# A recommender tower on one core: the first block of samples gets its own split of the pair units, the sums get freer groups, and the order is planned anew

## What is computed

```python
e = jnp.stack([tbl_0[ids[:, 0]], ..., tbl_39[ids[:, 39]]], axis=1)   # (2048, 40, 64)
viW = jnp.einsum('bpd,pde->bpe', vi, W)      # vi = e[:, i_idx], W is (780, 64, 64)
z = jnp.einsum('bpe,bpe->bp', viW, vj)       # (2048, 780)
h = jnp.concatenate([z, dense_ctx], axis=1)  # 16 dense columns more: 796
h = jnp.maximum(h @ W_top1 + b_top1, 0.0)    # 512
h = jnp.maximum(h @ W_top2 + b_top2, 0.0)    # 256
y = h @ W_top3                               # 1
```

## Time and profile before

| | |
|---|---|
| median of 3 runs | 1356.27 us (1356.18 to 1361.23) |
| profiled execution: from its first to its last instruction (the span) | 1195.2 us |
| difference of the median to that span | 161.1 us |
| PE busy | 1177.7 us (99%) |
| DVE busy | 1003.0 us (84%) |
| ACT busy | 966.7 us (81%) |
| POOL busy | 774.4 us (65%) |
| TensorE clock granted | full (1.000) all along |
| bytes moved | 79.73 MB, 67 GB/s over the span |

### The profile page before, as it was taken

One profiled execution on the slowest core, in us unless ns is written; L12 is line 12 of the kernel. 1 busy time (PEld: TensorE's weight loads), 2 busy tenths in 40 slices (PEclk: granted clock), 3 DMA queues, 4 the chain that ended last, 5 costly groups with the idle time before them and its releaser, 6 DMA issues.

```text
span 1195.2 us, 23954 instructions
## 1 busy us (share of the span) xinstructions
PE 1177.7 (99%) x6248; PEld 457.7 (38%) x6248; DVE 1003.0 (84%) x915; ACT 966.7 (81%) x7477; POOL 774.4 (65%) x1026
## 2 busy tenths in 40 slices
PE   7999999999999999999999999999999999999999
PEld 2433333333434343333434343433343434343333
DVE  7898999999588888999877878889978778888960
ACT  1295989899476799999687879999969899999971
POOL 8888883687656556677755557887765556634320
PEclk9999999999999999999999999999999999999999
DMA  7143232222222222222222222222222222211100
GB/s 211 38 148 78 65 75 65 70 72 72 57 56 68 56 67 73 68 67 70 71 55 63 60 64 65 71 63 78 73 57 59 59 66 63 66 45 55 49 10 0
DMA packets 68480, 79.73 MB, mean 67 GB/s; under 512 B 15308, under 2 KB 46028, under 8 KB 68216
## 3 DMA queue, kind: packets, MB, share of 16 engines
q1 hardware_dynamic: 48752, 58.10, 16.6%
q0 software_dynamic: 19456, 19.96, 9.3%
q10 hardware_dynamic: 136, 0.14, 0.1%
HBM read 78.14 MB, written 0.01 MB: 65 GB/s over the span
## 4 chain that ended last, share of the span: by engine, by line
PE 89%; DVE 5%; issue 4%; ACT 1%; POOL 1%; DMA 0%; SPq 0%; DVEq 0%; ACTq 0%; POOLq 0%
PE u_ps L1007 30%; PE u_ps L1003 23%; PE z_ps L1032 16%; PE turn_ps L1063 7%; PE turn_ps L965 3%; PE u_ps L997 3%; PE turn_ps L958 2%; DVE fprod L1172 2%; PE turn_ps L1073 2%; PE u_ps L1063 2%; DVE acts L1128 1%; DVE zb L1180 1%; DVE rprod_A L1163 1%; PE u_ps L1073 1%; ACT rprod_A L1234 1%
## 5 line engine op out<-in xcount | busy, mean ns | idle before, releaser
L1234 ACT ACTIVATE rprod_A<-rprod_A 128x64 f32<-128x64 f32 x3664 | 877.8, 243 | 95.2 <-DVE rprod_A L1163 66.5
L899 POOL DMA_INDIRECT rows<-in_tbl,ids_all x608 | 575.2, 946 | 288.6 <-issue 113.5
L1234 ACT ACTIVATION_READ_ACCUMULATOR rprod_A<-rprod_A 128x1 f32 x3664 | 691.6, 189 | 0.1
L1172 DVE TENSOR_TENSOR fprod<-u_ps,x 128x1024 f32<-128x1024 f32 x440 | 524.0, 1222 | 32.1 <-PE u_ps L1007 31.9
L1007 PE MATMUL u_ps<-x,wf_ring 64*128 64x512 f32 x1760 | 444.9, 604 | 2.3 <-DVE fprod L1172 0.7
L1163 DVE TENSOR_TENSOR rprod_A<-u_ps,rows 128x1024 f32<-128x1024 f32 x213 | 260.5, 1224 | 98.0 <-PE u_ps L1003 97.8
L1003 PE MATMUL u_ps<-wr_ring,x 64*128 64x512 f32 x1280 | 338.7, 614 | 0.1
L1007 PEld LDWEIGHTS u_ps<-x,wf_ring 64*128 64x128 f32 x1760 | 158.6, 186 | 219.4 <-issue 163.9
L1032 PE MATMUL z_ps<-fprod,ones 128*32 128x512 f32 x1760 | 212.4, 598 | 0.0
L919 POOL TENSOR_TENSOR rprod_P<-rprod_P 128x512 f32<-128x512 f32 (+4 forms) x235 | 142.5, 606 | 81.7 <-DVE rprod_P L1163 58.6
L1003 PEld LDWEIGHTS u_ps<-wr_ring,x 64*128 64x128 f32 x1280 | 110.2, 185 | 172.7 <-issue 92.8
(11 more groups left out here) (45 smaller groups left out, 299.4 us busy)
## 6 DMA issues: line engine op xcount, KB each, us to landing
wf_ring<-in_w_standing SPq DMA_DIRECT2D x220, 128.0 KB
wr_ring<-in_w_moving SPq DMA_DIRECT2D x80, 256.0 KB
rows<-in_tbl,ids_all POOLq DMA_INDIRECT x608, 2.5
mlp_sb<-in_mlp SPq DMA_DIRECT2D x1, 2308.0 KB
mlp_sb<-in_tbl SPq DMA_DIRECT2D x6, 224.0 KB
wi_ring<-in_w_inner SPq DMA_DIRECT2D x20, 64.0 KB, 1.8
rows<-in_first_ids SPq DMA_DIRECT2D x4, 256.0 KB, 6.2
rprod_P<-in_first_ids SPq DMA_DIRECT2D x4, 256.0 KB, 8.8
```

Source lines behind the costliest of these rows:

```text
L899: nc.gpsimd.indirect_dma_start(rows[:, v % ROW_SLOTS, s, par * DIM:(par + 1) * DIM], None, tables[f], bass.IndirectOffsetOnAxis(ap=ids_all ...
L1172: nc.vector.tensor_tensor(fprod[:, f % FPROD_SLOTS], u_ps[:, bank:bank + 2, :], other, ALU.mult).then_inc(prods_done, 1)
L1234: op = nc.scalar.activation(of[:, j, :], of[:, j, :], ACT.Copy, accum_out=sum_at(u, j))
```

## The change

It gives every block its own list `MOVED`, in a class `Shape`. Block 0 gets (0, 4, 3, 4, 6): 122 F units, and 73 R and I units. Blocks 1 to 3 get (0, 4, 5, 5, 12): 86 F units, and 109 R and I units. Altogether there are 380 F units (before: 440) and 400 R and I units (before: 340). z of block 0 has 4 + 3 chunks, that of the later blocks 3 + 4. As the rows of the layer 1 matrix stand in another order for the later blocks, its 3584 columns are loaded again once, by SP, at the first unit behind block 0's layer 1. The weights lie twice in DRAM, once for each kind of block.

Sums are no longer cut into fixed groups of 4 F units. A group has one or two halves (2 F units each), as many as are ready at the time (`sums_ready`, `SUM_MOST`). The planner's other rules and estimates change: the cost of turning between kinds of PE work, backlogs of two units for ACT and POOL, `ROWS_LEAD` 7 (5), `GAP` 0.2 (-0.3), steps of the layers at least 20 units apart where nothing waits (14), `zr` only when the layer 1 before it is done.

```diff
--- before.py
+++ after.py
-MOVED = [0, 3, 4, 5, 8]
+MOVED = [(0, 4, 3, 4, 6), (0, 4, 5, 5, 12), (0, 4, 5, 5, 12), (0, 4, 5, 5, 12)]
 FOLD = 2 * 8
-GROUP = 4
-HALF = GROUP // 2
+HALF = 2
...
+class Shape:
+    def __init__(self, moved):
+        self.moved = moved
+        self.standing = [("F", n, k) for n in range(DUOS) for k in range(moved[n // 4], n)]
+        self.chunks = [(q, k) for q in range(QUADS) for k in range(moved[q])]
+        self.moving = [unit for q in range(QUADS) for unit in
+                       [("R", c, s) for c, (of, _) in enumerate(self.chunks) if of == q for s in range(SUBS)]
+                       + [("I", q, 0)]]
+        self.nf, self.nr, self.nc = len(self.standing), len(self.moving), len(self.chunks)
+        self.halves, self.tiles = self.nf // HALF, 2 * self.nf
+        self.inner_at = sum(moved[:QUADS - 1])
+        self.zf = -(-self.tiles // Z_TILES)
+        self.r_pairs = self.nc * FOLD + DUOS
+        self.zr = -(-self.r_pairs // P)
+        self.zk = self.zf + self.zr
...
+KINDS = sorted(set(MOVED))
+SHAPES = [Shape(moved) for moved in MOVED]
+KIND_OF = [KINDS.index(moved) for moved in MOVED]
+ZK, ZR = max(shape.zk for shape in SHAPES), max(shape.zr for shape in SHAPES)
+Z_RING = 9 - ZR
+ZB_SLOTS = 5
...
-T_UNIT, T_SUMS, T_DUO, T_PASS, T_TURN = 0.846, 0.41 * GROUP, 0.44, 0.858, 0.17
-T_PROD, T_VSUM, T_PART, T_COPY, T_RELU = 1.131, 1.127, 0.48, 0.58, 0.69
-T_GATHER, T_ROWS, T_FOLD = 1.25, 2.5, 3.3
-T_PACE, PACE_OVER, AHEAD_OF = 1.6, 6, 1.0
+T_UNIT, T_ROUND, T_DUO, T_PASS = 0.858, 0.858, 0.49, 0.858
+T_TURN = {"main": {"sum": 0.10, "turn": 0.10}, "sum": {"main": 0.21, "turn": 0.10},
+          "turn": {"main": 0.21, "sum": 0.10}}
+T_PROD, T_VSUM, T_PART, T_COPY, T_RELU = 1.131, 1.131, 0.48, 0.58, 0.69
+T_GATHER, T_ROWS, T_FOLD = 1.25, 2.5, 3.65
+T_PACE, T_PACE_FIRST, PACE_OVER, AHEAD_OF = 1.6, 1.6, 6, 1.0
 LAG_PE, LAG_DVE, LAG_ACT, LAG_POOL = 0.225, 0.15, 0.09, 0.08
 T_FIRST = 4.3
-T_INNER = 1.75
+T_INNER = 1.78
 T_HOT, T_BUILD, T_TABLE, T_TABLES = 0.423, 0.535, 8.5, 1.6
-LEAD, LEAST, ROWS_LEAD = 8, 1, 5
-STALL, GAP = 0.05, -0.3
-MLP_GAP, MLP_PACE = 8, 14
-AHEAD, BEHIND = 2, 10
+LEAD, LEAST, ROWS_LEAD = 8, 1, 7
+STALL, GAP, SOON = 0.05, 0.2, 0.3
+MLP_GAP, MLP_PACE = 5, 20
+AHEAD, BEHIND = 2, 25
 BACK = 2
-A_MOST, P_MOST = 1, 1
+SUM_LEAST, SUM_MOST, SUM_WAIT, FOLLOW = 1, 2, 0.0, 0
+CHAIN = 0
+A_MOST, P_MOST, V_MOST = 2, 2, 2
...
+def z_before(b, k):
+    old = Z_FROM[b] + k - Z_RING
+    if old < 0:
+        return None
+    of = max(a for a in range(NB) if Z_FROM[a] <= old)
+    assert of < b or k >= SHAPES[b].zf
+    return of if of < b else None
...
+    def half_ready(self, b, h):
+        f = F_FROM[b] + HALF * h + HALF - 1
+        if f >= len(self.f_units):
+            return None
+        at = self.prod_at[self.f_units[f]]
+        return max(at, self.z_at[-1]) if h % Z_HALVES == 0 and self.z_at else at
+    def sums_ready(self, at):
+        if self.next_half() is None:
+            return 0
+        b, h = self.next_half()
+        n, stop = 0, min(SHAPES[b].halves, (h // Z_HALVES + 1) * Z_HALVES)
+        while h + n < stop:
+            ready = self.half_ready(b, h + n)
+            if ready is None or ready > at:
+                break
+            n, at = n + 1, at + T_ROUND
+        return n
+    def do_sums(self, n):
+        b, h = self.next_half()
+        self.order.append(("sum", b, h, n))
         t = self.pe_t + self.turn_to("sum")
-        if g % K_GROUPS == 0 and self.z_at:
-            t = max(t, self.z_at[-1])
-        for last in range(first + HALF - 1, NF * b + min(GROUP * (g + 1), NF), HALF):
-            t = max(t, self.prod_at[self.f_units[last]]) + T_SUMS / 2
+        for i in range(n):
+            t = max(t, self.half_ready(b, h + i)) + T_ROUND
             self.half_at.append(t + LAG_PE)
         self.pe_t, self.mode = t, "sum"
-        if g % K_GROUPS == K_GROUPS - 1 or g == GROUPS - 1:
-            k = g // K_GROUPS
+        end = h + n
+        if end % Z_HALVES == 0 or end == SHAPES[b].halves:
+            k = (end - 1) // Z_HALVES
             ready = self.half_at[-1]
-            if b and k == Z_SPARE:
-                ready = max(ready, self.done["l1", b - 1, M1 - 1])
+            if z_before(b, k) is not None:
+                ready = max(ready, self.done["l1", z_before(b, k), M1 - 1])
             self.z_at.append(self.do_act(("z", b, k), ready, T_COPY))
+        return b if end == SHAPES[b].halves else None
...
+    def must_step(self, steps, unit):
+        if unit and unit[1] != "F":
+            b = unit[0]
+            c = ZR_FROM[b] + SHAPES[b].first_column(*unit[1:3]) // P - ZB_SLOTS
+            if c >= 0 and ("zr", *ZR_CHUNKS[c]) not in self.done:
+                return True
+        if self.next_half() is None or not steps or steps[0][0] not in ("zr", "l1"):
+            return False
+        b, h = self.next_half()
+        old = z_before(b, h // Z_HALVES)
+        if old is None or ("l1", old, M1 - 1) in self.done or h % Z_HALVES < Z_HALVES - 4:
+            return False
+        return steps[0][0] == "zr" or self.step_ready(steps[0]) is not None
...
+    def choose(self, b, f, r):
+        shape, turned = SHAPES[b], len(self.turned_at)
+        f_known = f < shape.nf and self.need < turned
+        r_known = False
+        if r < shape.nr:
+            quad = DUOS * b + 4 * shape.quad_of(*shape.moving[r][0:2])
+            r_known = (DUOS * b + shape.stands(*shape.moving[r][0:2])[-1] < turned and
+                       self.arrived.get(quad + 3, 9e9) <= self.pe_t + 1)
+        due = (f - 4) * shape.nr / (shape.nf - 8) - r
+        relaxed = r_known and self.slot_free("A") <= self.pe_t + T_UNIT and len(self.parts) <= 6
+        if r_known and (not f_known or due > 0 or due > -AHEAD and relaxed):
+            if f_known and due < BEHIND and not relaxed and len(self.queue["V"]) > V_MOST:
+                return (b, *shape.standing[f])
+            return (b, *shape.moving[r])
+        return (b, *shape.standing[f]) if f_known else None
...
+                full = len(self.f_units) - FPROD_SLOTS
+                if self.must_step(steps, unit):
                     what = "step"
                 elif back and turned >= HOT and (stall > STALL or u >= BACK) and self.bank_at <= soon:
                     what = "back"
-                elif must_sum:
+                elif unit and unit[1] == "F" and full >= 0 and full // HALF >= len(self.half_at):
                     what = "sum"
                 elif unit is None:
-                    what = "duo" if duo_at is not None else "sum"
-                    if duo_at is not None and sums and sum_ready < duo_at - 1:
-                        what = "sum"
-                elif turned < base + DUOS + LEAD and duo_at is not None and duo_at <= soon and turned <= need + LEAST and (
-                        stall > STALL or turned <= need + 1 and f < NF and base + STANDING[min(f + 3, NF - 1)][1] >= turned):
+                    what = "sum" if duo_at is None or ready and duo_at > self.pe_t + 1 else "duo"
+                elif wanted and duo_at <= soon and turned <= self.need + LEAST and (
+                        stall > STALL or turned <= self.need + 1 and f < shape.nf and
+                        base + shape.standing[min(f + 3, shape.nf - 1)][1] >= turned):
                     what = "duo"
-                elif step_at is not None and u - last_step >= MLP_PACE and step_at <= soon and (stall > 0 or self.mode != "main"):
+                elif step_at is not None and u - step_u >= MLP_PACE and step_at <= soon and (
+                        stall > 0 or self.mode != "main"):
                     what = "step"
-                elif stall > STALL and sums and sum_ready <= soon:
+                elif self.mode == "turn" and FOLLOW and ready >= FOLLOW:
                     what = "sum"
-                elif stall > STALL and duo_at is not None and duo_at <= soon and turned <= need + LEAD:
+                elif self.mode != "main" and wanted and duo_at <= self.pe_t + 0.15 and turned <= self.need + CHAIN:
                     what = "duo"
-                elif stall > STALL and step_at is not None and step_at <= soon and u - last_step >= MLP_GAP:
+                elif stall > STALL and ready >= SUM_LEAST:
+                    what = "sum"
+                elif stall > STALL and wanted and duo_at <= soon and turned <= self.need + LEAD:
+                    what = "duo"
+                elif stall > STALL and step_at is not None and step_at <= soon and u - step_u >= MLP_GAP:
                     what = "step"
                 else:
                     what = "unit"
                 if what == "sum":
-                    sb, sg = sums.pop(0)
-                    self.do_sums(sb, sg)
-                    if sb == b - 1 and sg == GROUPS - 1:
-                        mlp[len(mlp) - ZR:len(mlp) - ZR] = tail_of(sb)
+                    summed = self.do_sums(min(max(1, ready), SUM_MOST))
...
```

(64 more changed lines are left out.)

358 lines of the change are left out of this document (166 added, 192 removed).

## The result

| | before | after |
|---|---|---|
| median of the runs | 1356.22 us (1355.35 to 1361.23) | 1311.65 us (1310.65 to 1312.93) |
| profiled execution, span | 1195.2 us | 1311.1 us |

The ratio is 0.9669 (95% interval 0.9649 to 0.9689): 44.6 us or 3.3% faster. The forecast was 1338 us, a gain of 18.5 us, and the range 1320 to 1356. The direction was right, the size was not, and the two spans say at once that a premise was wrong. The profiled run after took 1312.93 us, only 1.8 us more than its span. So nothing like 161 us lies around a span, and the first profile of before shows an execution that took about 1197 us, which none of the timed runs repeated.

A forecast was written before the change was run, and what follows sets the result against it. The prediction took PE's work as the bound, in block 0 also DVE's pace. Its terms, -25.8 + 2.3 + 5.0 + 0 = -18.5 us, took the span from 1195.2 to 1176.7 and the median to 1338 us, range 1320 to 1356.

The forecast's parts named there:

- Sums that go: On PE, 60 F units lose their product with ones, at 0.43 us each: -25.8 us.
- zb chunks and insertions: On PE, three more chunks to turn, +2.3 us, and 127 groups of sums instead of 112, +5.0 us.
- The price of 0.33 us: On PE, what every insertion between units costs beyond the sums themselves (0.10 + 0.13 + 0.10).
- 1.5 halves a group: Assumed size of PE's sum groups: 190 halves make 127 groups, +15 x 0.33 = +5.0 us.
- rival B: Insertions on PE eat the gain: 170 groups (+19.1 us), waits as in the forecast, 1352 us; chance 0.14.
- Waits of PE for DVE: Block 0's waits fall from 12 to 5 us (-7), the others' rise from 8 to 15 (+7): together 0.
- Rival C: DVE becomes the bound in blocks 1 to 3, from about 35 reductions a block: 1370 us; chance 0.09.
- waits off DVE's load: PE's waits taken from DVE's load: 5 us at 90% in block 0, 5 each at 90 to 93% in the others.
- The reload: 1.84 MB in SP's queue behind block 0's layer 1: cost 0, at most 5 us if the R ring runs dry.
- Outside the span: Median less profiled span, 161.1 us (1356.3 - 1195.2), nothing in the trace prices them; taken as they are.
- Rival A: PE's sum groups stay large (100, -4.0 us) and waits small (-8.0 us): 1321 us; chance 0.12.
- D: The reload starves a ring, 5 us in one place: 1343 us; chance 0.05.

The follow-up runs named there:

- fill_before: Kernel before with each of the 608 gathers replaced by a constant fill on POOL, same place, waits and semaphores: 1197.83 us.
- fill_after: Kernel after with each gather replaced by a constant fill on POOL, same place, waits and semaphores: 1171.66 us.
- before_again: Kernel before, unchanged, run and profiled again: 1355.52 us; the profiled execution took 1349.83 us, its span is 1347.7 us.
- pause_long: Kernel after with the fill between two gathers of block 0 twice as wide (128x512), a gather every 1.65 us: 1226.67 us, ratio 0.9227.
- fill_old_split: Kernel after with the old split of 110/85 in all four blocks and its gathers replaced by fills: 1197.56 us.
- old_split: Kernel after with the old split of 110/85 in all four blocks, new planner and sum groups kept: 1337.24 us, ratio 0.9884.
- before_long: Kernel before with the wider fill (128x512) between block 0's gathers: 1284.26 us, ratio 0.9481.
- old_split_long: Kernel after with the old split of 110/85 in all four blocks and the wide fill (128x512) in block 0: 1266.54 us, ratio 0.9353.
- groups2: Kernel after with `SUM_LEAST` 2 for 1, so 96 sum groups in place of 143: 1328.77 us, ratio 0.9814.
- gap_later: pause_long with a fill of 128x256 on POOL behind each gather of blocks 1 to 3 too: 1229.62 us, ratio 0.9082.
- pause_two: Kernel after with two fills of 128x512 behind each gather of block 0, a gather every 2.23 us: 1312.34 us, ratio 0.9673.

## Why the prediction was wrong

PE's work can be added up from the timelines with the prices of the prediction, piece by piece; what is left over is waiting. So "sums" and "other work" are counts times prices, and an error of a price would stand under "waits". For the spans, in us:

| | sums | other work, switching | waits of PE |
|---|---|---|---|
| fill_before | 188.7 | 245.4 | 21.8 |
| fill_after | 163.0 | 256.3 | 10.5 |
| before_again | 188.7 | 245.4 | 174.9 |
| after | 163.0 | 256.3 | 152.9 |
| pause_long | 163.0 | 256.3 | 60.3 |

(The units, the table products and what lies ahead of them are left out, 739 to 740 us, in pause_long 744, as its first product comes 5 us later. The first profile of before is as fill_before.)

- **Sums that go: -25.8 forecast, -25.7 by the count.** Right.
- **zb chunks and insertions: +2.3 + 5.0 forecast, +10.9 by the count.** The price of 0.33 us held. The number was 143 groups (96 of one half, 47 of two), between the 127 of the forecast and the 170 of rival B, so the choice of 1.5 halves a group mis-sized this term by 16 groups, 5 us. The sum is off by 1.7 us less than that: 12 groups stand directly ahead of turning work (before: 3), which saves a change each time.
- **Waits of PE for DVE: 0 forecast, -11.3 without gathers.** Block 0's went from 14 to 1.6 (forecast 12 to 5), the other blocks' from 8 to 9 (forecast 8 to 15). DVE did 12, 35, 34 and 20 reductions (forecast 10, 29, 29, 20), as POOL took 10 in blocks 1 and 2 and not 16: more than I gave it, and still with fewer waits. Rival C had put the point from which DVE decides at about 35, and blocks 1 and 2 reached it without that. The step that failed is the one that read waits off DVE's load ("for 90% in block 0 I take 5, for 90 to 93% in the others 5 each"). fill_old_split, which has block 0's 25 reductions as before, waits there 9.7 and not 14, so most of that fall is the split's. In the later blocks the new order alone brings the waits from 8 down to about 2, and the split brings them back to 9. That small groups, inserted at the moment PE catches up, are what keeps the two in step at 93% is an argument; no run without gathers had other groups.
- **The reload: 0 forecast.** Right without gathers: fill_after lands it in 7.3 us, and PE waits there for no load but the tables'. The order of transfers that the Trainium skill names ("DMA: Bandwidth & Descriptors", section "Two DMAs through the same engine are not ordered") cost nothing that shows.
- **Outside the span: "161.1 us, I take them as they are".** This is the step that failed worst. Around the span lie 1.8 us (after) and 2.1 (before_again), and the rest was inside, as waits. The median was to be set against the profiled execution's own time, and the page had only its span; a gap of 12% should have been read as two different executions. 153 us of it are waits that only executions with the hold-up have. Nor did the term stay as it was: from the kernel without gathers to the kernel with them it is 158 us before and 140 after (medians, on several chips).

So of the 44.6 us some 26 are what the forecast was about, where it said 18.5, and the other 18 are less hold-up. The stretches say the same: forecast were about 267, 281, 275 and 275 us for the four blocks, and they are 267, 281, 277 and 268 in fill_after, but 357, 294, 302 and 282 in the kernel after. The ledger has PE's waits in ordinary executions fall by 22 us, where they fall by 11 without gathers (the profile of before_again is of an execution 6 us under the median). That it is the new order and not the split that lessens the hold-up is shown twice (old_split, 16 to 20 us; before_long to old_split_long, 17). Which of its rules does it isn't: groups2 shows that small groups are worth 17 us with the gathers in, the others weren't tried by themselves. Nor is it settled what in the chip an indexed DMA holds up, why the one execution escaped it, and why the hold-up sets in between 1.65 and 1.44 us a gather.

Rival A had the nearest time of all (1321, too high by 9), and that is luck: its small waits (-8) did come, at -11, but the groups were not large, and it too took the 161.1 us as they were. Rivals B, C and D are out: there were 143 groups and not 170, DVE had 101 reductions and not 111 and was not the bound, and no ring ran dry at the reload.

pause_long and gap_later beat both kernels: their ratios to the kernel before are 0.9227 and 0.9082, that of the kernel after is 0.9669. fill_after shows that another 55 us would be had if the gathers held up nothing.

## What to carry to other kernels

Before a forecast is built on a profile, hold its span against the timed runs: if they differ by more than a few us, the profile is of another execution, and the largest cost may be one that it doesn't show. If all engines but one slow down together while none names what it waits for, take away what that one engine does, by a cheap stand-in with the same semaphores; then vary its pace, and read after each step whether the waits left are still the unnamed ones: pause_two is as slow as the kernel after for quite another reason. An engine off the critical path (POOL here, 59% busy) can cost 150 us without a single wait that names it.

## What the runs showed of the hardware that was not expected

- Indexed DMAs of 128 rows, issued by POOL every 1.44 us, slowed PE, DVE and ACT to a quarter to two fifths in stretches of block 0. Plain DMAs of 128 neighbouring rows did not (1183.9 us, against 1313.2 with neighbouring rows by index).
- ACT took 2 to 3 activations a gather in place of 6. Waits that the profile can't name reached 12.0 us on DVE and 12.7 on ACT. In the one followed here, PE's count of finished units reached DVE and SP at 92.42 us, for a unit begun at 77.77.
- 0.2 us more between the gathers of one block was worth 4.4 points of the ratio, about 60 us (85 by the medians). DVE's unnamed waits in that block were 105.8, 66.6, 7.9 and 9.2 us with a gather every 1.25, 1.44, 1.65 and 2.23 us.
- PE's clock dropped to the 1.2 GHz level in these stretches (0.50 granted from 63 to 66 us, 0.66 from 60 to 100), after PE had begun to idle; in pause_long, it stayed at 1.00.
